# Three fp32r passes for the nearest Toeplitz tiles of a convolution, and where on the engines their operands are split

## The chip, the cores and the metric

The kernel runs on one core of a Trainium2 chip, in one launch. The metric is the time of the whole execution on the device, in microseconds (us). Five engines work side by side, each through its own instructions in order: TensorE (PE) multiplies matrices into PSUM, VectorE (DVE), ScalarE (ACT) and GpSimd (POOL) compute element by element, and SyncE (SP) issues DMA transfers.

## The reference, cut to what matters

```python
def reference(x, lengths, cond, ...):        # x: 32 batches, 64 channels, 1024 positions
    # 1. a long convolution per channel, by FFT, with a mask of lengths
    u_m = x * mask[:, None, :]
    K[h, l] = 2 * Re(sum_n Cs[h, n] * exp(dtA[h, n] * l))      # 64 modes, l = 0..1023
    y = irfft(rfft(u_m, n=2 * L) * rfft(K, n=2 * L), n=2 * L)[..., :L]
    y = (y + u_m * D[:, None]) * mask[:, None, :]
    # 2. grouped attention with rope on y: q, k, v products, softmax, output product
    x = x + attention(y, Wq, Wk, Wv, Wo)
    # 3. a product per batch with a chosen 64x64 matrix, then a feed-forward of experts
    return x + moe_lora(einsum("bct,bcd->bdt", x, W[cond]), W_base, gate_W, A, B)
```

Everything is float32. The change concerns part 1 alone.

## The kernel before

The convolution of a channel is a product with a Toeplitz matrix: y[t] is a sum of K[t - s] x[s]. Positions are cut into 8 blocks of 128; the tile of distance d (0 to 7) joins each block of x with the block d further on, and serves all (8 - d) x 32 columns (block and batch) at once. Each tile is cut into two halves c of 64 input positions. That makes 16 tiles (d, c), the list TILES; the nearer the distance, the more columns: 256, 256, 224, 224, 192, 192, and so on down to 32, 32.

**Steps.** The stage has 32 steps n of two channels each (S // 2). Channel r = 0 takes partitions 0 to 63 of the array's input, r = 1 takes 64 to 127, so that two matmuls run side by side. The first nine tiles are WIDE: 64 inputs x 128 outputs, two matmuls each (`wide`, L644). The other seven are NARROW: two halves of 64 outputs as well, four matmuls each (`narrow`, L654). All are fp32, which the trace shows as two records for each matmul. Even steps run WIDE and then NARROW, odd steps NARROW (and tile (0, 0) in narrow form) and then the rest of WIDE (`convolve`, L668). Four steps are a group (GP); kernels of the convolution are computed by groups.

**Rings.** Toeplitz rows of a step (`toep`, 544 columns) lie in a ring of three: SyncE may load those of step n when step n - 3 has ended (`load_toeplitz`, L615, four transfers; the rows come from `kpad` in DRAM, where ScalarE has stored the kernels). x of two steps (`xc`) lies in a ring of two, loaded ahead of the rows of an even step (`load_x_conv`, L587). PSUM has three slots. SyncE also loads a piece of the weights for the products that follow, in steps 5 to 16.

**Behind the matmuls of step n.** VectorE multiplies by the mask of lengths into `ym` (L740). ScalarE rounds it to fp32r into `y_hi` (L771, L772). GpSimd subtracts to get `y_lo` (L783, L784). Products later in the kernel run as three fp32r passes, high x high, high x low and low x high (PASSES), on such pairs.

**Kernels of the convolution**, two groups ahead, for the first six groups: GpSimd makes exponents (L392), VectorE phases after the mask of the group's first step (L463, L467, L474), ScalarE exponentials and sines in the second step, with a table load before each kind (L357, L373), VectorE tables in the third, TensorE the kernel product after the fourth (L543, in the first group within step 1 too), VectorE takes it out (`kernels_out`), and ScalarE stores it at the head of the group that follows (`store_kernels`, four DMA issues, L573).

The order on each engine is that in which the code is written: `conv_loads`, `conv_matmuls`, `conv_masks`, `conv_hi` and `conv_lo` each run their engine's loop over n. An engine that waits at one instruction runs none behind it.

## Time and profile before

| | |
|---|---|
| median of three runs | 877.52 us (876.6 to 879.48) |
| the profiled execution | 876.56 us, span 874.7 us |
| TensorE busy | 854.1 us (98%) |
| VectorE, ScalarE, GpSimd busy | 467.1, 221.4, 450.0 us |
| granted TensorE clock | 1.00 |
| convolution | up to 164.4 us of the span |

The profile is one execution. Busy time of TensorE counts overlapping records once, and says little of how near it is to its peak; the beat of a stage is read from when its pieces start, in the timeline. The chain of waits follows the work that ended last backward. A wait in it counts only if nothing else would have ended as late.

### The profile page before, as it was taken

The numbers are of one execution on the slowest core, as the hardware profiler recorded it, in microseconds if no ns is written. First come the engines' busy times: TensorE is split into PE (matmuls) and PEld (weight loads), VectorE is DVE, ScalarE is ACT, GpSimd is POOL, SyncE is SP. The second block draws the span as 40 slices with busy tenths as digits, with TensorE's granted clock in tenths as the row PEclk, the third lists the DMA queues.
The fourth block names the chain that finished last, engine by engine and source line by source line (L and its number), as shares of the span: only waits on it lengthen the run. The fifth ranks groups of instructions, "written<-read, shape, count | busy, mean of one in ns | idle before, by whom it ended". The sixth has DMA issues, their size and how long they took to land.

```text
span 874.7 us, 24616 instructions
## 1 busy us (share of the span) xinstructions
PE 854.1 (98%) x10866; PEld 741.9 (85%) x10866; DVE 467.1 (53%) x898; ACT 221.4 (25%) x377; POOL 450.0 (51%) x346
## 2 busy tenths in 40 slices
PE   3999999999999999999999999999999999999998
PEld 2899999988888888887777777777779999999998
DVE  7555651122522222238887777888854755545444
ACT  4445552100000000013132333333334322211220
POOL 3344555302367555649978888877746422102220
PEclk9999999999999999999999999999999999999999
DMA  3788877413354322255534454545437211222211
GB/s 95 177 207 220 208 186 196 162 60 127 109 183 129 82 74 73 50 166 154 142 129 149 135 176 165 173 163 173 151 123 234 96 59 57 83 97 97 98 49 49
DMA packets 97339, 114.90 MB, mean 131 GB/s; under 512 B 44112, under 2 KB 66896, under 8 KB 97232
## 3 DMA queue, kind: packets, MB, share of 16 engines
q1 hardware_dynamic: 94240, 112.29, 43.1%
q8 instruction: 86, 1.41, 0.7%
q10 hardware_dynamic: 2480, 0.51, 0.3%
q0 software_dynamic: 512, 0.53, 0.2%
q14 instruction: 21, 0.17, 0.1%
HBM read 80.16 MB, written 33.13 MB: 130 GB/s over the span
## 4 chain that ended last, share of the span: by engine, by line
PE 93%; SPq 3%; DMA 2%; DVE 1%; issue 0%; ACT 0%
PE ps L988 25%; PE ps L1275 21%; PE ps L1597 15%; PE ps L649 8%; PE ps L1625 5%; PE ps L952 5%; PE ps L660 4%; PE ps L1231 3%; PE ps L1211 3%; PE ps L1507 2%; SPq L606 2%; DMA toep<-kpad 2%; PE ps L1642 1%; PE ps L1641 1%; DMA kpad<-ksb 1%
## 5 line engine op out<-in xcount | busy, mean ns | idle before, releaser
L1597 PE MATMUL ps<-wb_hi,xf 128*128 128x424 f32 x440 | 127.0, 356 | 0.0
L988 PE MATMUL ps<-y_hi,w_hi 128*128 128x512 f32 x320 | 125.1, 391 | 0.0
L988 PE MATMUL ps<-y_hi,w_lo 128*128 128x512 f32 x320 | 124.5, 389 | 0.0
L988 PE MATMUL ps<-y_lo,w_hi 128*128 128x512 f32 x320 | 124.5, 389 | 0.0
L1573 POOL TENSOR_TENSOR xf<-xs,xf 128x512 fp32r<-128x512 f32 x32 | 42.1, 1347 | 124.8 <-DVE xs L1561 124.8
L1275 PE MATMUL ps<-y_hi 128*128 128x512 f32 x256 | 102.9, 402 | 0.0
L1275 PE MATMUL ps<-y_hi,y_lo 128*128 128x512 f32 x256 | 100.2, 391 | 0.0
L1275 PE MATMUL ps<-y_lo,y_hi 128*128 128x512 f32 x256 | 100.1, 391 | 0.0
L649 PE MATMUL ps<-xc,toep 64*128 64x192 f32 (+4 forms) x1088 | 97.1, 330 | 2.5 <-DMA toep<-kpad 2.4
L649 PEld LDWEIGHTS ps<-xc,toep 64*128 64x128 f32 x1088 | 91.2, 187 | 6.0 <-issue 3.8
L1597 PEld LDWEIGHTS ps<-wb_hi,xf 128*128 128x128 f32 x440 | 82.7, 188 | 2.3
L1100 POOL TENSOR_TENSOR rot<-rot,cst 128x512 f32<-128x512 f32 x40 | 52.8, 1319 | 58.7 <-DVE rot L1070 58.7
L1303 POOL TENSOR_TENSOR sc<-sc,stat 128x1024 f32<-128x1024 f32 x32 | 62.0, 1937 | 38.8 <-DVE stat L1299 38.8
L1597 PE MATMUL ps<-wb_lo,xf 128*128 128x424 f32 x220 | 77.6, 353 | 0.0
L1070 DVE LOAD_MASK_SELECT rot<-ps x40 | 0.6, 14 | 134.1 <-PE ps L988 119.1
L988 PEld LDWEIGHTS ps<-y_hi,w_hi 128*128 128x128 f32 x320 | 60.1, 188 | 12.8
L988 PEld LDWEIGHTS ps<-y_hi,w_lo 128*128 128x128 f32 x320 | 60.1, 188 | 12.5
L988 PEld LDWEIGHTS ps<-y_lo,w_hi 128*128 128x128 f32 x320 | 60.1, 188 | 12.3
L1317 POOL TENSOR_TENSOR sc<-sc,stat 128x1024 f32<-128x1024 f32 x32 | 66.8, 2086 | 2.2 <-DVE stat L1313 2.2
L783 POOL TENSOR_TENSOR y_lo<-ym,y_hi 128x256 fp32r<-128x256 f32 x32 | 30.3, 946 | 70.0 <-ACT y_hi L772 69.8
L1104 POOL TENSOR_TENSOR rf<-rot,rc 128x512 f32<-128x512 f32 x40 | 52.7, 1317 | 17.2 <-DMA k_rows<-rf 14.1
L820 ACT ACTIVATE w_hi<-wraw 128x1024 fp32r<-128x1024 f32 (+1 forms) x11 | 12.4, 1137 | 186.6 <-PE ps L988 108.8
(190 smaller groups left out, 1624.3 us busy)
## 6 DMA issues: line engine op xcount, KB each, us to landing
toep<-kpad SPq DMA_DIRECT2D x124, 136.0 KB
xc<-in_dram SPq DMA_DIRECT2D x32, 256.0 KB, 4.4
q_rows<-rf SPq DMA_DIRECT2D x32, 256.0 KB, 2.8
q<-q_rows SPq DMA_DIRECT2D x16, 512.0 KB, 3.9
xr<-in_dram SPq DMA_DIRECT2D x16, 512.0 KB, 4.4
x_scratch<-xr SPq DMA_DIRECT2D x16, 512.0 KB, 3.0
x<-x_scratch SPq DMA_DIRECT2D x16, 512.0 KB, 4.3
out_dram<-x SPq DMA_DIRECT2D x15, 512.0 KB, 2.9
```

Source lines behind the costliest of these rows:

```text
L649: mm = pe.matmul(ps[:, 2 * (n % 3) + r, d * NB:NJ * NB], toep[rows, n % TR, at:at + P], xc[rows, n // XH % XR, 1 - c, n % XH, 0:(NJ - d) * ...
L660: mm = pe.matmul(ps[half * HALF:(half + 1) * HALF, 2 * (n % 3) + r, d * NB:NJ * NB], toep[rows, n % TR, at:at + HALF], xc[rows, n // XH % ...
L952: mm = pe.matmul(out, wv[a][:, j, h * P:(h + 1) * P], y[b][:, j, b0:b1, s0:s1], start=(j == 0 and a + b == 0), stop=(j == NJ - 1 and a == 1))
L988: mm = pe.matmul(kq_bank(n), w[a][:, j, :], yt[b][:, j, g * 512:(g + 1) * 512], start=(j == 0 and a + b == 0), stop=(j == NJ - 1 and a == 1))
L1100: gp.tensor_tensor(r, r, across(C("sin"), 8), ALU.mult).then_inc(g_rsin, 1)
L1104: gp.tensor_tensor(rf[:, (NVB + n) % SR, :], rot[:, n % RR, :], rc[:, n % RR, :], ALU.add).then_inc(g_rsum, 1)
L1275: mm = pe.matmul(ps[:, 6 + n, :], heads, wo(c, t)[:, n, :], start=(at == 0), stop=(at == 3 * NQT - 1))
L1303: gp.tensor_tensor(sc_groups(u), sc_groups(u), along(stat[:, u % CR, 0, :], S), ALU.subtract).then_inc(g_sub, 1)
L1317: gp.tensor_tensor(sc_groups(u), sc_groups(u), along(stat[:, u % CR, 2, :], S), ALU.mult).then_inc(g_prob, 1)
L1573: gp.tensor_tensor(xf(i, op, 1)[:], xs(i, op), xf(i, op, 0)[:].bitcast(F32), ALU.subtract).then_inc(g_xflo, 1)
L1597: mm = pe.matmul(dst[:, PLAIN:], xf(i, idx, a)[:, t, :], wb(c, idx, t), start=(start and t == 0 and a + c == 0), stop=(t == 3 and a == 1), ...
L1625: mm = pe.matmul(plain_bank[:, k, :], xf(i, op, a)[:, t, :], w[c][:, first + t, :], start=(op in (A11, S1) and t + a + c == 0), stop=(op i ...
```

## The change

The four tiles of the two nearest distances (NEAR = 4: (0,0), (0,1), (1,0), (1,1)) run from step 2 on as three fp32r passes (`near_tiles`). For this, x and the first 320 columns of the Toeplitz rows of a step are split in two parts each. `near_hi` on ScalarE copies x (once `xc` has landed) and the rows (once `toep` has landed) to fp32r; `near_lo_x` on VectorE and `near_lo_rows` on GpSimd subtract. `near` holds two steps of rows, `xs_pair` two steps of x; the latter lies in the third slot of the split weights, and so the first key weights are loaded after the convolution. The scratch of the start shares memory with `near`.

The parts for step n + 2 are made in step n. For an odd n (and n = 0) they stand behind y_hi and y_lo of step n. For an even n from 2 on they stand ahead of mask, y_hi and y_lo of step n, and ScalarE waits there for `pe_near`, which TensorE raises after the near passes of step n. On TensorE the near passes stand between WIDE and NARROW in an even step, and at the end of an odd step.

Pieces of value weights are now loaded in steps 15 to 22 (W_FIRST = 16) and rounded in step 25; VectorE subtracts their low part, in steps 27 and 29, in place of GpSimd.

```diff
-        W_FIRST = 6
+        W_FIRST = 16
...
+        NEAR_COLS = 2 * P + HALF
+        near = [sb(f"near_{n}", [P, 2, NEAR_COLS], F32R, s1) for n in ("hi", "lo")]
...
+        xs_pair = [w[:, WR - 1, :].rearrange("p (r c n) -> p r c n", r=2, c=2) for w in wsp]
...
+        def near_tiles(pe, n):
+
+            pe.wait_ge(a_near, 2 * (n - FIRST_NEAR + 1))
+            pe.wait_ge(g_near, n - FIRST_NEAR + 1)
+            pe.wait_ge(v_near, n - FIRST_NEAR + 1)
+            for d, c in TILES[:NEAR]:
+                at = d * P + (1 - c) * HALF
+                for a, b in PASSES:
+                    for r in range(2):
+                        rows = slice(r * HALF, (r + 1) * HALF)
+                        mm = pe.matmul(ps[:, 2 * (n % 3) + r, d * NB:NJ * NB], near[a][rows, n % 2, at:at + P],
+                                       xs_pair[b][rows, n % 2, 1 - c, 0:(NJ - d) * NB],
+                                       start=False, stop=True, skip_group_check=True)
+            return mm
...
-            if n % 2 == 0:
+            if n >= FIRST_NEAR and n % 2 == 0:
+                for d, c in WIDE[NEAR:]:
+                    wide(pe, n, c, d, start=((d, c) == WIDE[NEAR]), stop=True)
+                near_tiles(pe, n).then_inc(pe_near, 1)
+                for d, c in NARROW:
+                    mm = narrow(pe, n, c, d, start=False, stop=True)
+            elif n >= FIRST_NEAR:
+                for d, c in NARROW:
+                    narrow(pe, n, c, d, start=((d, c) == NARROW[0]), stop=True)
+                for d, c in WIDE[NEAR:]:
+                    wide(pe, n, c, d, start=False, stop=True)
+                mm = near_tiles(pe, n)
+            elif n % 2 == 0:
...
+                if n + 1 == FIRST_NEAR or n % 2 == 0 and n >= FIRST_NEAR:
+                    near_lo_x(v, n + 1)
+                if near_early(n):
+                    near_lo_x(v, n + AHEAD)
+                if n in (W_FIRST + 11, W_FIRST + 13):
+                    value_weight_lo(v, (n - W_FIRST - 11) // 2)
                 v.wait_ge(pe_conv, n + 1)
...
+        def near_made(n):
+
+            return FIRST_NEAR <= n + AHEAD < S // 2
+
+        def near_early(n):
+
+            return near_made(n) and n % 2 == 0 and n >= FIRST_NEAR
+
+        def near_hi(act, n):
+            if near_early(n - AHEAD):
+                act.wait_ge(pe_near, (n - AHEAD - FIRST_NEAR) // 2 + 1)
+            act.wait_ge(ld_xc[n // XH % XR], 16 * 2 * (n // XH // XR + 1))
+            act.activation(xs_pair[0][:, n % 2, :, :], xc[:, n // XH % XR, :, n % XH, :], ACT.Copy).then_inc(a_near, 1)
+            act.wait_ge(ld_toep[n % TR], rows_landed(n))
+            act.activation(near[0][:, n % 2, :], toep[:, n % TR, 0:NEAR_COLS], ACT.Copy).then_inc(a_near, 1)
...
-                if n == W_FIRST + 13:
-                    weight_hi(act, 0)
+                if near_early(n):
+                    near_hi(act, n + AHEAD)
                 act.wait_ge(v_mask, n + 1)
                 act.activation(y_pair(0, n, 0), ym_pair(n, 0), ACT.Copy)
                 act.activation(y_pair(0, n, 1), ym_pair(n, 1), ACT.Copy).then_inc(a_yhi, 1)
+                if near_made(n) and not near_early(n):
+                    near_hi(act, n + AHEAD)
                 if n == 0:
                     store_kernels(act, 1)
...
+                if near_early(n):
+                    near_lo_rows(gp, n + AHEAD)
                 gp.wait_ge(a_yhi, n + 1)
                 gp.tensor_tensor(y_pair(1, n, 0), ym_pair(n, 0), y_pair(0, n, 0).bitcast(F32), ALU.subtract)
                 gp.tensor_tensor(y_pair(1, n, 1), ym_pair(n, 1), y_pair(0, n, 1).bitcast(F32), ALU.subtract).then_inc(g_ylo, 1)
...
+                if near_made(n) and not near_early(n):
+                    near_lo_rows(gp, n + AHEAD)
```

What stands in a row on ScalarE from the head of a group (step 8) to its second step. Before (L573 stores kernel rows, L771 and L772 are y_hi, L357 exponentials, L373 sines):

```order
L573 DMA kpad<-ksb 32x2x32 [waits v_k]
L573 DMA kpad<-ksb 32x2x32 x3
L771 ACTIVATE y_hi<-ym 128x256 [waits v_mask]
L772 ACTIVATE y_hi<-ym 128x256
L357 ACT_TABLE_LOAD
L357 ACTIVATE mg<-mg 128x256 [waits g_mag] x2
L373 ACT_TABLE_LOAD
L373 ACTIVATE rn<-rn,cst 128x256 [waits v_round]
L373 ACTIVATE rn<-rn,cst 128x256 x2
L771 ACTIVATE y_hi<-ym 128x256 [waits v_mask]
L772 ACTIVATE y_hi<-ym 128x256
```

And now, where L582 is the store, L843 and L844 are y_hi, L366 and L382 exponentials and sines, and L812 and L814 are the two copies of `near_hi`:

```order
L582 DMA kpad<-ksb 32x2x32 x3
L812 ACTIVATE w12_hi<-xc 128x512 [waits ld_xc1,pe_near]
L814 ACTIVATE near_hi<-toep 128x320 [waits ld_toep1]
L843 ACTIVATE y_hi<-ym 128x256 [waits v_mask]
L844 ACTIVATE y_hi<-ym 128x256
L366 ACT_TABLE_LOAD
L366 ACTIVATE mg<-mg 128x256 [waits g_mag] x2
L382 ACT_TABLE_LOAD
L382 ACTIVATE rn<-rn,cst 128x256 [waits v_round]
L382 ACTIVATE rn<-rn,cst 128x256 x2
L843 ACTIVATE y_hi<-ym 128x256 [waits v_mask]
L844 ACTIVATE y_hi<-ym 128x256
```

The copies for step 10 have come ahead of y_hi of step 8, with waits for two loads; those for step 11 stand behind y_hi of step 9. On GpSimd the same stretch, from the exponents (L401) on, where L823 is `near_lo_rows` and L859 and L860 are y_lo:

```order
L401 TENSOR_TENSOR mg<-t64,cst 128x256 [waits g_rtab,v_tab]
L401 TENSOR_TENSOR mg<-t64,cst 128x256
L823 TENSOR_TENSOR near_lo<-toep,near_hi 128x320 [waits a_near]
L859 TENSOR_TENSOR y_lo<-ym,y_hi 128x256 [waits a_yhi]
L860 TENSOR_TENSOR y_lo<-ym,y_hi 128x256
L859 TENSOR_TENSOR y_lo<-ym,y_hi 128x256 [waits a_yhi]
L860 TENSOR_TENSOR y_lo<-ym,y_hi 128x256
L823 TENSOR_TENSOR near_lo<-toep,near_hi 128x320 [waits a_near] x2
```

Before, the exponents and the y_lo pairs stood there alone; now the low rows of the odd step stand behind y_lo of the second step of the group.

## Rows read from the trace of the kernel before

**Rows 1.** The page, the chain that ended last: share of the span by engine
```profile
PE 93%; SPq 3%; DMA 2%; DVE 1%; issue 0%; ACT 0%
```

**Rows 2.** Timeline of PE: start us, length us, engine, line, operation, shapes, count
```profile
40.42 0.61 PE L543 MATMUL ps<-ph 64*128 64x128 f32 x8
...
68.09 3.31 PE L649 MATMUL ps<-xc,toep 64*128 64x256 f32 x36 [0.93 <-DMA toep<-kpad]
...
83.07 5.96 PE L649 MATMUL ps<-xc,toep 64*128 64x256 f32 x68
...
112.48 3.20 PE L649 MATMUL ps<-xc,toep 64*128 64x256 f32 x36
...
126.64 2.87 PE L649 MATMUL ps<-xc,toep 64*128 64x256 f32 x32
129.35 0.61 PE L543 MATMUL ps<-ph 64*128 64x128 f32 x8
129.80 3.20 PE L649 MATMUL ps<-xc,toep 64*128 64x256 f32 x36
...
161.53 2.87 PE L649 MATMUL ps<-xc,toep 64*128 64x256 f32 x32
```

**Rows 3.** Waits of PE from 28 to 170 us: sum, times, longest
```profile
PE ps L649 <- DMA toep<-kpad: 2.2, 3, 1.1
```

**Rows 4.** The chain in order of time: start us, length us, what
```profile
27.92 3.83 DMA toep<-kpad
...
138.44 0.63 SPq L593
...
141.71 5.21 DMA toep<-kpad
...
147.05 3.31 PE ps L649 x36
```

**Rows 5.** Timeline of ACT, steps 11 to 14, columns as in rows 2
```profile
77.56 0.65 ACT L771 ACTIVATE y_hi<-ym 128x256 fp32r<-128x256 f32 x1 [3.14 <-DVE ym L740]
78.02 0.64 ACT L772 ACTIVATE y_hi<-ym 128x256 fp32r<-128x256 f32 x1
78.56 2.91 ACTq L573 DMA_DIRECT2D kpad<-ksb  x4
...
83.62 1.28 ACT L357 ACT_TABLE_LOAD   x1
...
88.60 0.67 ACT L772 ACTIVATE y_hi<-ym 128x256 fp32r<-128x256 f32 x1
...
91.87 1.92 ACT L820 ACTIVATE w_hi<-wraw 128x2048 fp32r<-128x2048 f32 x1
```

**Rows 6.** Timelines of DVE (first line) and of POOL, same stretch
```profile
81.76 0.69 DVE L740 TENSOR_TENSOR ym<-ps,valid 128x512 f32<-128x512 f32 x1 [3.24 <-PE ps L660]
...
89.34 1.08 POOL L783 TENSOR_TENSOR y_lo<-ym,y_hi 128x256 fp32r<-128x256 f32 x1 [3.84 <-ACT y_hi L772]
90.36 0.95 POOL L784 TENSOR_TENSOR y_lo<-ym,y_hi 128x256 fp32r<-128x256 f32 x1
...
98.11 2.36 POOL L824 TENSOR_TENSOR w_lo<-wraw,w_hi 128x1024 fp32r<-128x1024 f32 x1
```

**Rows 7.** Timeline of PE, value products: the first and the last of 58
```profile
165.04 0.28 PE L952 MATMUL ps<-y_hi,w_lo 128*128 128x256 f32 x1
...
171.89 0.28 PE L952 MATMUL ps<-y_hi,w_lo 128*128 128x256 f32 x1
```

**Rows 8.** Timeline of ACT, steps 0 and 1
```profile
29.39 2.17 ACTq L573 DMA_DIRECT2D kpad<-ksb  x4
31.59 1.28 ACT L357 ACT_TABLE_LOAD   x1 [4.61 <-issue]
...
36.57 0.68 ACT L772 ACTIVATE y_hi<-ym 128x256 fp32r<-128x256 f32 x1
```

More of the change, by code:

```diff
@@ L155, in build @@
         ksb = sb("ksb", [P, 2, 2, GP * HB], F32, s1)
+        first = ExitStack()
+        prm = sb("prm", [P, 5, S], F32, first)
+        t64_first = sb("t64_first", [P, 18, S], F32, first)
+        first.close()
+        NEAR_COLS = 2 * P + HALF
+        near = [sb(f"near_{n}", [P, 2, NEAR_COLS], F32R, s1) for n in ("hi", "lo")]
         s1.close()
+        xs_pair = [w[:, WR - 1, :].rearrange("p (r c n) -> p r c n", r=2, c=2) for w in wsp]
         s2 = ExitStack()
@@ L288, in build @@
             "a_set", "v_set", "v_rho", "v_ang", "v_cs")]
-        g_zero, v_cidx, v_len, v_valid = [signal(n) for n in (
-            "g_zero", "v_cidx", "v_len", "v_valid")]
-        g_set, g_den, g_fac, g_rtab = [signal(n) for n in ("g_set", "g_den", "g_fac", "g_rtab")]
+        g_zero, v_cidx, v_valid = [signal(n) for n in (
+            "g_zero", "v_cidx", "v_valid")]
+        g_set, g_fac, g_rtab = [signal(n) for n in ("g_set", "g_fac", "g_rtab")]
         g_mag, a_mag, v_ph, v_round, a_sin, v_tab = [signal(n) for n in (
@@ L297, in build @@
             "pe_conv", "v_mask", "a_yhi", "g_ylo")]
-        a_whi, g_wlo, pe_unit = [signal(n) for n in (
-            "a_whi", "g_wlo", "pe_unit")]
+        pe_near, a_near, v_near, g_near = [signal(n) for n in (
+            "pe_near", "a_near", "v_near", "g_near")]
+        a_whi, g_wlo, v_wlo, pe_unit = [signal(n) for n in (
+            "a_whi", "g_wlo", "v_wlo", "pe_unit")]
         pe_v, v_v = signal("pe_v"), signal("v_v")
@@ L638, in conv_loads @@
                 part, piece = divmod(n - W_FIRST + 1, W_PIECES)
-                if 0 <= part < 3:
+                if 0 <= part < 2:
                     cols = slice(piece * W_COLS, (piece + 1) * W_COLS)
-                    source = w_v[:, part * NJ * P:(part + 1) * NJ * P] if part < 2 else w_qk[0]
-                    sp.dma_start(wraw[:, part, cols], source[:, cols]).then_inc(ld_w[part // 2 * 2], 16)
+                    source = w_v[:, part * NJ * P:(part + 1) * NJ * P]
+                    sp.dma_start(wraw[:, part, cols], source[:, cols]).then_inc(ld_w[0], 16)
         def wide(pe, n, c, d, start, stop=False):
@@ L650, in wide @@
                                xc[rows, n // XH % XR, 1 - c, n % XH, 0:(NJ - d) * NB],
-                               start=start, stop=stop)
+                               start=start, stop=stop, skip_group_check=(n >= FIRST_NEAR and not start))
             return mm
@@ L661, in narrow @@
                                    xc[rows, n // XH % XR, 1 - c, n % XH, 0:(NJ - d) * NB],
-                                   start=start, stop=stop)
+                                   start=start, stop=stop, skip_group_check=(n >= FIRST_NEAR and not start))
             return mm
@@ L666, in build @@
         WIDE, NARROW = TILES[:NJ + 1], TILES[NJ + 1:]
+        FIRST_NEAR = 2
+        AHEAD = 2
+        NEAR = 4
+        def near_tiles(pe, n):
[11 more added lines that the diff above has]
+            return mm
         def convolve(pe, n):
@@ L752, in ym_pair, with near_lo_x, near_lo_rows @@
             return ym[:, n % 2, i, :].rearrange("p (j b) -> p j b", b=NB)
+        def near_made(n):
[9 more added lines that the diff above has]
+            act.activation(near[0][:, n % 2, :], toep[:, n % TR, 0:NEAR_COLS], ACT.Copy).then_inc(a_near, 1)
+        def near_lo_x(v, n):
+            v.wait_ge(a_near, 2 * (n - FIRST_NEAR) + 1)
+            v.tensor_tensor(xs_pair[1][:, n % 2, :, :], xc[:, n // XH % XR, :, n % XH, :],
+                            xs_pair[0][:, n % 2, :, :].bitcast(F32), ALU.subtract).then_inc(v_near, 1)
+        def near_lo_rows(gp, n):
+            gp.wait_ge(a_near, 2 * (n - FIRST_NEAR) + 2)
+            gp.tensor_tensor(near[1][:, n % 2, :], toep[:, n % TR, 0:NEAR_COLS],
+                             near[0][:, n % 2, :].bitcast(F32), ALU.subtract).then_inc(g_near, 1)
         def conv_hi(act):
@@ L799, in w_loaded @@
             s = w_slot(m).start
-            pieces = (2 * W_PIECES, 0, W_PIECES)[s]
-            whole = 0 if m <= 0 else (m - 1) // WR + 1 if s == 0 else m // WR + (s == 1)
+            pieces = (2 * W_PIECES, 0, 0)[s]
+            whole = 0 if m < 0 else (m - 1) // WR + 1 if s == 0 else m // WR + 1
             eng.wait_ge(ld_w[s], 16 * (pieces + whole))
@@ L811, in load_weights @@
             if w_users(m) > 0:
-                sp.wait_ge(g_wlo, w_users(m))
+                sp.wait_ge(v_wlo, 2)
+            if w_users(m) > 1:
+                sp.wait_ge(g_wlo, w_users(m) - 1)
             s = w_slot(m).start
@@ L820, in weight_hi, with value_weight_lo @@
             act.activation(wsp[0][:, w_slot(m), :], wraw[:, w_slot(m), :], ACT.Copy).then_inc(a_whi, 1)
-        def value_weight_lo(gp, part):
-            gp.wait_ge(a_whi, 1)
-            return gp.tensor_tensor(wsp[1][:, part, :], wraw[:, part, :], wsp[0][:, part, :].bitcast(F32), ALU.subtract)
+        def value_weight_lo(v, part):
+            v.wait_ge(a_whi, 1)
+            v.tensor_tensor(wsp[1][:, part, :], wraw[:, part, :], wsp[0][:, part, :].bitcast(F32), ALU.subtract).then_inc(v_wlo, 1)
         def weight_lo(gp, m):
@@ L884, in qkv_transfers @@
         def qkv_transfers(sp):
+            load_weights(sp, 0)
             load_weights(sp, 1)
```

33 lines of the change are left out of this document (14 added, 19 removed).

## The prediction

> **What bounds the kernel now.** I read first the chain of work that ended last: TensorE holds nearly all of it [rows 1], and the convolution is its stretch up to 164.4 us. The timeline of TensorE gives that stretch its beat [rows 2]. One group of four steps is the time from one kernel-row product (L543, which follows the last step of a group) to the next: 40.42 to 129.35 holds five groups, (129.35 - 40.42) / 5 = 17.8 us each, and a pair of steps takes some 8.65 us. TensorE is almost never idle there: its waits in the whole stage sum to 2.2 us, none over 1.1 [rows 3]. So the stage looks bound by matmuls. But two things stand close behind. The rows of a Toeplitz tile for step n+2 are asked for when step n-1 ends and land 8.5 us later (138.44 to 141.71 + 5.21 = 146.92, step 28 starts at 147.05) [rows 4]: a pair of steps shorter than that waits for its load. And ScalarE does, in the second step of each group of the first six, the tables, exponentials and sines of the kernels two groups on: from 83.62 to 88.60 + 0.67 = 89.27 it holds y_hi of step 13 back, 5.65 us in all; the subtractions of GpSimd for that step follow until 91.31 [rows 5, 6]. In the kernel before nobody waits for that: y_lo is needed only two steps later.
>
> **What TensorE gains.** Per step from 2 on, four wide fp32 tiles (256, 256, 224, 224 columns, 960 in sum, two row halves side by side) go, and 24 fp32r matmuls come: 12 pairs. Old price: 68 records over 3328 columns take 5.96 us [rows 2], so 960 columns take 1.72 at most; four cycles a column at 2.4 GHz are 1.60. I take 1.64. New price: no fp32r matmul on half rows stands in the trace. The nearest row is the one on full rows, 256 columns: from 165.04 to 171.89 lie 57 of them, 0.120 us apart, that is 106.7 ns of columns and 13 ns more [rows 7]. If the two halves overlap as the fp32 ones do, the pass costs 3 x (2 x 0.120 + 2 x 0.107) = 1.36; without the 13 ns 1.20. If they don't overlap, 2.72. I take 1.36, since the fp32 tiles of this very shape do run as pairs. The gain is 0.28 a step, 1.1 us a group, 8.4 us over 30 steps if nothing else spoke.
>
> **What the split costs on the other engines.** Each step adds on ScalarE a copy of 512 columns and one of 320 (from 1.92 us for 2048 columns and 0.65 for 256 strided ones [rows 5]: about 0.6 and 0.45), on VectorE one subtraction of 512 columns (as the mask, 0.69 [rows 6]), on GpSimd one of 320 (2.36 us for 1024 [rows 6], so 0.74). Their busy time fits. Their place doesn't. On ScalarE the copies for an even step n+2 stand ahead of y_hi of step n, and the second waits for the Toeplitz rows of n+2. Those land 7.1 to 8.5 us after step n-1 ended (3.27 of issuing, then the 3.83 to 5.21 us of landing shown [rows 4]), about when step n+2 starts. ScalarE stands still until then; in the kernel before y_hi of step n ran just as step n ended. Behind it are queued, in the same order: y_hi of n, the tables, exponentials and sines, y_hi of n+1, and only then the copies for the odd step n+3; on GpSimd y_lo of n+1 stands ahead of the low part of those rows. TensorE needs that low part in the fourth step of the group.
>
> I follow this ring for a group, from the end e of the step before it (4g-1):
> - The mask and y_hi of 4g-1 (0.7 + 1.1), copies for 4g+1 (1.0), four stores of kernel rows (2.9 [rows 5]) fill ScalarE until e + 5.8; then the copy of x for 4g+2, VectorE's subtraction and the mask of step 4g end at e + 7.9. The rows land at e + 7.1 to 8.5 and are copied 0.5 later. So y_hi of 4g starts between e + 7.9 and e + 9.0. I take 8.3, below the middle: while step 4g-1 waits, its loads and those before it have landed, and the transfers have less to share with.
> - y_hi of 4g: 1.10 (77.56 to 78.66). Tables to y_hi of 4g+1: 5.65. [rows 5]
> - y_lo of 4g+1: 1.97 (89.34 to 91.31) [rows 6], and 0.07 of signal.
> - Low part of the rows of 4g+3: 0.74 + 0.05. Near passes of 4g+3, which end the step: 1.36 + 0.05.
>
> Sum: 8.3 + 1.10 + 5.65 + 2.04 + 0.79 + 1.41 = **19.3 us a group** (18.8 to 20.2), against 17.8 before. TensorE's own work would be 17.3 less 1.1 (the group 112.48 to 129.80 is one without a wait), 16.2 to 16.6; it waits about 3 us in the fourth step, ahead of its near passes. Since the ring is longer than the matmuls, their gain doesn't count in it but for the pass at its end.
>
> **The start.** The copies for step 2 stand ahead of the store of the second group of kernel rows, and their rows land at 27.92 + 3.83 = 31.75 [rows 4]. ScalarE then goes on at 32.25; the stores (2.17, begun at 29.39 before) end at 34.45, tables to y_hi of step 1 take 31.59 to 36.57 + 0.68 = 5.66, to 40.1 [rows 8]; y_lo of step 1 as above 2.04, to 42.1; low rows of step 3 to 42.9, near passes to 44.35. Step 3 ended at some 40.6 before (the kernel product behind it stands at 40.42 [rows 2]): +3.8 us. The kernel rows of group 1 are stored 2.9 us later, and so the rows of step 4 land 2.9 later; that hides in it.
>
> **The rest of the stage.** After step 23 there are no exponentials and sines left. Eight steps took 161.53 + 2.87 = 164.4 less 126.64 + 2.87 = 129.5, that is 34.9 [rows 2]; less 8 x 0.28 is 32.6, but a pair of 8.08 us stands against a load of up to 8.5, and a load that is asked for a pair ahead holds two pairs to their mean, (8.08 + 8.5) / 2 = 8.3: 33.2. The rounding of the value weights (1.92) falls in step 25; the ring of that group, 8.3 + 1.1 + 1.9 + 1.1 + 2.0 + 0.8 + 1.4 = 16.6, just ties with matmuls. Gain -1.6. Weight pieces of other steps, and the first key weights, now loaded after the convolution, lie under the 44 us of value products; the change leaves y of step 31 as far ahead of its reader as it was.
>
> **Sum.** End of step 3 +3.8; five groups 5 x (19.3 - 17.8) = +7.6; the last eight steps -1.6: **+9.8 us**. The profiled execution took 876.56 (span 874.7 and 1.9 around it), the median of the runs shown is 877.52, 1 us over it. The span comes to 884.5, the median to 877.5 + 9.8 = **887.3 us**.
>
> **Rivals.**
> 1. *The beat is TensorE's after all* (faster). If the rows landed some 3 us earlier than here, or if ScalarE had 3 us less, the ring would be below 16.4 and each pair bound by matmuls or loads: 15 pairs, 8.65 down to 8.3, and the first group 1 to 2 us late: 877.5 - 5.3 + 1 = 873 us. For it: TensorE's own work does shrink. Against: it takes 3 us out of a ring of which each term but the first has a row. It decides at a ring of 17.8. Chance 0.11. Between, with a ring of about 17.6 to 18.4 (copies and landings all at their short end): 876 to 881, chance 0.09.
> 2. *The halves don't overlap.* Near pass 2.72: a step takes 4.33 - 1.64 + 2.72 = 5.4, a group 21.7 with its kernel product, which beats the ring (20.7). Step 3 ends 1.4 later, five groups 5 x 3.9 = 19.5, the last eight 8 x 1.08 = 8.7: 877.5 + 5.2 + 19.5 + 8.7 = 911. Against: the fp32 pairs of this shape. Chance 0.06. The Trainium skill ("TensorE: Matmul & The Clock Gate", LDWEIGHTS and "The mechanism") gives a load of 128 columns 107 ns and lets it overlap a running matmul where the row group differs; by that each half would alternate load and matmul, some 0.2 us a pair, and the time would be near this rival's. The rows on full rows speak against it: 0.120 us from one fp32r matmul to the next, each with a weight load of its own [rows 7].
> 3. *The clock.* TensorE now stands idle 3 to 4.5 us once a group; the longest wait of the stage before was 1.1 us [rows 3], at clock 1.00. If the clock falls from 2.4 to 1.2 GHz, the near pass behind the gap doubles, +1.4 us on the ring, while the slower steps after it fit in the slack; at most six times 1.4, 896 us. Chance 0.10. The same page of the skill says that idle TensorE is throttled to half rate; no row of this trace shows it either way.
> 4. *Same*, by cases that cancel: within rival 1's middle.
>
> **Chances.** Forecast (ring 18.4 to 20.2, 882 to 893) 0.64, rival 1 0.11, its middle 0.09, rival 2 0.06, rival 3 0.10. What a measurement tells from no change is 0.3%, 2.6 us. Faster 0.11, same 0.07, slower 0.82. The range of 8 in 10 takes the forecast, the clock up to 896 and the middle down to 879: 879 to 896.
>
> **What would show it.** In the changed profile: TensorE's wait in the fourth step of groups 0 to 5, ahead of the near passes, on GpSimd's low rows, some 3 us, and 4 in step 3; none later. ScalarE's copy of near rows for even steps waiting for the load for 1 to 3 us. L552 to L552 19.3 us instead of 17.8. Near passes of 24 matmuls in 1.36 us. Wrong if the gaps are missing (then rival 1), if the passes take 2.7 us, or if a clock under 1.00 stands in the slices.

## The result, and the profile after

The changed kernel took 899.57 us (median of 4 runs, 898.39 to 904.24), beside 877.62 us for the kernel before (median of 4): the ratio is 1.025, with an interval of 1.021 to 1.029. That is 22 us slower, and 3.6 us above the upper end of the range. The execution that was profiled took 904.24 us, the longest of the four, with a span of 901.9. The kernel was run and profiled once more later on (`again` below: 897.88 us, its profiled span 895.1), and where the two profiles differ both are given.

The waits of TensorE from 20 to 200 us (sum, times, longest), to be held against [rows 3]:

```profile
PE ps L691 <- POOL near_lo L823: 16.3, 5, 4.5
PE ps L669 <- issue: 3.8, 2, 2.8
PE ps L658 <- DMA toep<-kpad: 1.6, 2, 1.3
PE ps L691 <- issue: 1.4, 1, 1.4
```

Before, no wait of the stage was longer than 1.1 us, and all were for a load. Now TensorE waits five times, 16.3 us in sum, for the low part of the Toeplitz rows that GpSimd makes (L823), and each of these waits stands ahead of the near passes (L691) in the fourth step of a group. This is the gap that the prediction places there. The waits named "issue", for which the profile finds no releaser, are new, and they are of two kinds. The one at L691 (1.4 us) is the sixth wait for low rows: TensorE goes on at 64.61, 0.07 us after GpSimd's low rows end, as it does behind the other five. Those at L669 stand inside runs of narrow matmuls, where no semaphore is waited for; the part on `inter` below takes them up.

The chain of one group in order of time (start, length, what), to be held against [rows 4] and [rows 5]. The group starts at e = 108.75, where the kernel product ahead of it begins:

```profile
109.03 0.63 SPq L602
...
112.29 4.55 DMA toep<-kpad
...
116.86 0.47 ACT near_hi L814
117.33 0.58 ACT y_hi L843
...
118.39 1.28 ACT L366
...
119.68 0.73 ACT mg L366 x2
...
120.43 1.28 ACT L382
...
121.72 1.31 ACT rn L382 x3
...
124.09 1.09 POOL y_lo L859
125.19 1.30 POOL y_lo L860
126.49 1.27 POOL near_lo L823
...
127.85 2.91 PE ps L691 x24
```

The order is that of the ring, link by link: the loads are issued when the fourth step ends, the last rows land at e + 8.1, near_hi (the copy of the rows) is followed by y_hi, the table loads, exponentials and sines, y_hi of the next step, y_lo and low rows on GpSimd, and then the 24 near matmuls. These took 2.91 us here; where TensorE ran at full clock they took 1.45 to 1.55 (from their first start to the start of what follows).

The page's row of the granted clock (tenths of full speed in 40 slices of 22.5 us) shows two slices below the others in the convolution; before, all forty were alike:

```profile
PEclk9999998989999999999999999999999999999999
```

At the finer grain of the trace the clock goes down to 1.2 GHz six times between 42 and 193 us, for 3.4 or 6.8 us each, 30.7 us in sum: once at the end of each of the five waits of the first row or just behind it, and once behind this wait in the midst of the narrow matmuls of the last steps (start, length, line; the idle time ahead in brackets):

```profile
181.78 2.02 PE L669 MATMUL ps<-xc,toep 64*64 64x128 f32 x94
186.57 0.74 PE L669 MATMUL ps<-xc,toep 64*64 64x64 f32 x18 [2.77 <-issue]
```

In `again` the same kernel spent 17.1 us at 1.2 GHz in four places, behind gaps of 4.5, 2.6, 4.2 and 2.5 us but not behind those of 1.4 and 1.8, and had no such stall in its last steps. The starts of the kernel products (L552) there give the length of the groups, as in [rows 2]:

```profile
46.14 1.11 PE L552 MATMUL ps<-ph 64*128 64x128 f32 x8
...
66.05 0.65 PE L552 MATMUL ps<-ph 64*128 64x128 f32 x8
...
87.57 1.15 PE L552 MATMUL ps<-ph 64*128 64x128 f32 x8
...
107.41 0.65 PE L552 MATMUL ps<-ph 64*128 64x128 f32 x8
...
128.50 1.15 PE L552 MATMUL ps<-ph 64*128 64x128 f32 x8
...
149.51 1.15 PE L552 MATMUL ps<-ph 64*128 64x128 f32 x8
```

| us | before | forecast | after | again |
|---|---|---|---|---|
| end of step 3 (start of L552) | 40.4 | 44.35 | 46.4 | 46.1 |
| a group, mean of five | 17.8 | 19.3 | 21.1 | 20.7 |
| last eight steps | 34.8 | 33.2 | 40.6 | 34.5 |
| span | 874.7 | 884.5 | 901.9 | 895.1 |

For `again`: 5.7 + 5 x 2.9 - 0.3 = 19.9 us of the 20.4 us between the spans. So all but 0.5 us is found inside the convolution.

### The profile page after: what moved, and what is told of

Its sections match the earlier page's. It is cut to its first block, busy times and chain, and to the rows that moved or that the text cites. A ratio compares the mean times of both kernels' runs of the same rounds, so it can differ in the third digit from the quotient of the medians.

```text
span 901.9 us, 25138 instructions
## 1 busy us (share of the span) xinstructions
PE 860.9 (95%) x11046; PEld 751.4 (83%) x11046; DVE 502.3 (56%) x930; ACT 249.5 (28%) x437; POOL 483.1 (54%) x374
## 4 chain that ended last, share of the span: by engine, by line
PE 85%; DMA 4%; ACT 4%; SPq 3%; POOL 2%; DVE 1%; issue 1%; ACTq 0%
PE ps L1063 24%; PE ps L1352 20%; PE ps L1674 14%; PE ps L1702 5%; PE ps L1027 5%; PE ps L691 3%; PE ps L1308 3%; PE ps L1288 3%; DMA toep<-kpad 3%; PE ps L658 2%; PE ps L1584 2%; SPq L615 2%; PE ps L669 1%; PE ps L1719 1%; PE ps L1718 1%
## 5 line engine op out<-in xcount | busy, mean ns | idle before, releaser
L658 PE MATMUL ps<-xc,toep 64*128 64x192 f32 (+4 forms) x668 | 61.2, 330 | 1.6 <-DMA toep<-kpad 1.6
L658 PEld LDWEIGHTS ps<-xc,toep 64*128 64x128 f32 x668 | 56.7, 204 | 3.3 <-issue 2.6
L1845 DVE TENSOR_TENSOR x<-ps,x 128x424 f32<-128x424 f32 (+1 forms) x64 | 40.3, 642 | 33.9 <-PE ps L1674 31.8
```

Source lines behind the costliest of these rows:

```text
L658: mm = pe.matmul(ps[:, 2 * (n % 3) + r, d * NB:NJ * NB], toep[rows, n % TR, at:at + P], xc[rows, n // XH % XR, 1 - c, n % XH, 0:(NJ - d) * ...
L1845: v.tensor_tensor(x, src[:, first:], x, ALU.add).then_inc(v_sum_out, 1)
```

## The experiments

Each kernel ran beside the kernel before on its chip. "Over before" is the ratio less one, times 877.5 us, so that rows of different chips can be compared. The last three columns are read from the profiled execution as in the table above; that of `nosplit_spread` was the longest of its six, 885.4 us beside a median of 880.0.

| kernel | us | ratio [interval] | over before | end of step 3 | group | last eight |
|---|---|---|---|---|---|---|
| changed kernel | 899.6 | 1.025 [1.021, 1.029] | +21.9 | 46.4 | 21.1 | 40.6 |
| again | 897.9 | 1.0247 [1.0221, 1.0274] | +21.7 | 46.1 | 20.7 | 34.5 |
| late | 895.0 | 1.0214 [1.0166, 1.0261] | +18.8 | 45.1 | 20.0 | 36.8 |
| copy | 892.6 | 1.014 [1.0088, 1.0191] | +12.3 | 42.9 | 19.5 | 40.7 |
| nolowx | 897.3 | 1.0229 [1.0205, 1.0253] | +20.1 | 45.4 | 20.1 | 38.8 |
| fill | 901.0 | 1.0284 [1.023, 1.0338] | +24.9 | 45.7 | 21.7 | 34.2 |
| fill4 | 899.1 | 1.0264 [1.0243, 1.0286] | +23.2 | 45.0 | 21.4 | 34.1 |
| fill3 | 900.1 | 1.0256 [1.0236, 1.0276] | +22.5 | 44.9 | 20.7 | 34.7 |
| nosplit | 882.9 | 1.0077 [1.0053, 1.01] | +6.8 | 45.6 | 17.4 | 35.4 |
| nosplit_spread | 880.0 | 1.0041 [1.0021, 1.0062] | +3.6 | 45.9 | 17.8 | 37.3 |
| inter | 886.1 | 1.0097 [1.0061, 1.0133] | +8.5 | 40.5 | 19.5 | 35.7 |
| spread | 882.9 | 1.008 [1.006, 1.01] | +7.0 | 41.8 | 18.8 | 33.5 |
| spread2 | 886.3 | 1.0082 [1.0053, 1.011] | +7.2 | 40.5 | 19.4 | 35.2 |
| cut | 907.6 | 1.0357 [1.0339, 1.0374] | +31.3 | 44.2 | 21.7 | 43.1 |

### Is the splitting the cause: nosplit

```diff
+            made = min(n - FIRST_NEAR + 1, 2)
...
+            pe.wait_ge(g_near, made)
...
         def near_made(n):
...
-            return FIRST_NEAR <= n + AHEAD < S // 2
+            return FIRST_NEAR <= n + AHEAD < FIRST_NEAR + 2
...
         def near_early(n):
...
-            return near_made(n) and n % 2 == 0 and n >= FIRST_NEAR
+            return False
```

> The changed kernel with the fp32r operands made for steps 2 and 3 alone and used again in all later steps, so the products of the near distances are those of other data: ScalarE, VectorE and GpSimd do no splitting from step 4 on, TensorE's work is the same. Ring theory: without the copies the ring is shorter than TensorE's work; no wait for low rows, the clock stays at 1.00, 15 pairs at 8.3 us, 873 us (871 to 877). Rival (TensorE's own new work, its instruction supply or the loads set the beat): waits named issue stay and it is near 895 to 899.

It took 882.9 us, 6.8 over before, where the ring theory said 873 (871 to 877) and its rival 895 or more: neither number. The waits of TensorE:

```profile
PE ps L692 <- POOL near_lo L822: 4.0, 1, 4.0
PE ps L658 <- DMA toep<-kpad: 3.3, 5, 1.0
PE ps L669 <- issue: 2.0, 3, 1.3
```

TensorE does all its new work here, and 15 of the 22 us are gone: the splitting on the other engines costs them. The wait for low rows is left in step 3 alone, whose operands are still made (end of step 3 at 45.6, +5.2). From there on a group takes 17.4 us. The matmuls of a pair of steps run in 7.94 us (wide 1.34 and 1.44, near 1.55 and 1.45, narrow 2.16 together, taken from the trace) against 8.43 before, so four steps and the kernel product could be done in 16.4. The loads and the waits named issue keep the rest: what TensorE saves turns mostly into waits. So even without any splitting the change would be worth 2 us over the five groups, where rival 1, with 0.35 us a pair, has 3.5.

### Which link of the ring: late, copy, nolowx

`late` puts the splits of even steps behind y_hi and y_lo as well, the half of the change that its title names second undone (the low part of x moves with them):

```diff
-                if n + 1 == FIRST_NEAR or n % 2 == 0 and n >= FIRST_NEAR:
+                if near_made(n - 1):
                     near_lo_x(v, n + 1)
-                if near_early(n):
-                    near_lo_x(v, n + AHEAD)
...
         def near_early(n):
-            return near_made(n) and n % 2 == 0 and n >= FIRST_NEAR
+            return False
```

> The changed kernel, but the splits for every step, even or odd, stand behind the high and low part of y (the other half of the change's title undone; the wait on the near passes goes with it). Ring theory: ScalarE makes y_hi of step 4g before it waits for the rows of step 4g+2, so the ring is shorter by one y_hi, 1.1 us: about 20.0 us a group instead of 21.1, 893 us (888 to 896). The wait for GpSimd's low rows in the fourth step stays, some 2 us. Rival (the beat is TensorE's or the loads'): no change, 899.

895.0 us. By time alone it is not told apart from the changed kernel (the intervals of the ratios overlap); by the trace it is. y_hi of step 4g starts at e + 5.4 (e + 6.8 in the first of the five groups) instead of 8.4, the low rows are ready at e + 17.9 on the mean, against 18.97 in `again`, and the group is 0.7 us shorter (20.0, as forecast). TensorE's waits are divided among several causes, none over 1.9 us but the one in step 3:

```profile
PE ps L691 <- DVE w_lo L816: 5.6, 5, 1.5
PE ps L669 <- issue: 5.2, 3, 1.9
PE ps L691 <- POOL near_lo L821: 3.9, 1, 3.9
PE ps L691 <- issue: 2.8, 4, 1.0
```

`copy` makes plain copies of the exponentials and sines of groups 2 to 7, which leaves the table loads out:

```diff
-                act.activation(mg[:, i, :], mg[:, i, :], ACT.Exp).then_inc(a_mag, 1)
+                act.activation(mg[:, i, :], mg[:, i, :], ACT.Copy if g >= 2 else ACT.Exp).then_inc(a_mag, 1)
...
+                if step > 2:
+                    act.activation(rn[:, i, part], rn[:, i, part], ACT.Copy).then_inc(a_sin, 1)
```

> The changed kernel with the exponentials and sines of groups 2 to 7 replaced by plain copies on ScalarE, so no function tables are loaded there (two loads of 1.28 us a group) and the later kernel rows are wrong numbers. Ring theory: 2.6 us less between y_hi of 4g and y_hi of 4g+1, the low rows of 4g+3 ready at e + 16.3 instead of 18.9, the pass behind them at 2.4 GHz 1.55 us: 18.0 us a group instead of 21.1, and 2.6 less before step 3: 884 us (880 to 889). Rival (the ring isn't ScalarE's; loads or instruction supply set 20 us a group): 893 or more.

892.6 us, 9.6 us less than the changed kernel by the ratios where 15.6 were forecast: above the theory's range, which ended at 889, and close to the 893 of its rival. The start gained 3.2 us. In a group the low rows were ready at e + 17.6, not 16.3, because ScalarE now waits for VectorE (its timeline, with the idle time in brackets):

```profile
90.73 0.72 ACT L366 ACTIVATE mg<-mg 128x256 f32<-128x256 f32 x2
93.51 1.03 ACT L383 ACTIVATE rn<-rn 128x256 f32<-128x256 f32 x3 [2.05 <-DVE rn L486]
```

The sines need the phases that VectorE makes behind the mask of 4g, and the mask stands behind the low part of x for 4g+2, which waits for a load. In the changed kernel these phases end at 121.04, 0.7 us before ScalarE has its second table loaded (120.43 + 1.28, in the chain above). Take the loads away, and VectorE is the link in their place. So ScalarE's tables are one link of the ring, and not the only one that sets its length.

`nolowx` takes VectorE's added subtractions away from step 4 on, and TensorE's wait for them:

```diff
-            pe.wait_ge(v_near, n - FIRST_NEAR + 1)
+            pe.wait_ge(v_near, min(n - FIRST_NEAR + 1, 2))
...
-                if n + 1 == FIRST_NEAR or n % 2 == 0 and n >= FIRST_NEAR:
+                if n + 1 == FIRST_NEAR or n == 2:
                     near_lo_x(v, n + 1)
-                if near_early(n):
-                    near_lo_x(v, n + AHEAD)
```

> The changed kernel without VectorE's low part of x from step 4 on (that of steps 2 and 3 is used again, so the third product of the near passes is of other data). In the changed kernel VectorE makes the low parts of x for 4g+3 and 4g+4 while GpSimd makes y_lo of 4g+1 and the low rows, and these take 2.42 and 1.31 us where the forecast had 2.04 and 0.79. Contention theory: 1.97 and 0.87 again, the low rows ready at e + 18.1 instead of 18.95, 19.9 us a group, 895 us (893 to 897). If GpSimd's operations take that long by themselves: 899.

The timelines of GpSimd and, last row, of VectorE in `again`, where y_lo of 4g+1 (L859, L860) and two low rows (L823) run beside two low parts of x:

```profile
123.12 1.08 POOL L859 TENSOR_TENSOR y_lo<-ym,y_hi 128x256 fp32r<-128x256 f32 x1 [3.95 <-ACT y_hi L844]
124.15 1.35 POOL L860 TENSOR_TENSOR y_lo<-ym,y_hi 128x256 fp32r<-128x256 f32 x1
125.46 2.14 POOL L823 TENSOR_TENSOR near_lo<-toep,near_hi 128x320 fp32r<-128x320 f32 x2
...
123.51 2.55 DVE L818 TENSOR_TENSOR w_lo<-xc,w_hi 128x512 fp32r<-128x512 f32 x2
```

And GpSimd in `nolowx` (y_lo L857 and L858, low rows L821):

```profile
119.92 1.07 POOL L857 TENSOR_TENSOR y_lo<-ym,y_hi 128x256 fp32r<-128x256 f32 x1 [3.83 <-ACT y_hi L842]
120.94 0.90 POOL L858 TENSOR_TENSOR y_lo<-ym,y_hi 128x256 fp32r<-128x256 f32 x1
121.79 0.87 POOL L821 TENSOR_TENSOR near_lo<-toep,near_hi 128x320 fp32r<-128x320 f32 x1
```

y_lo takes 1.94 us instead of 2.4, the low rows 0.87 instead of 1.3 (means of five groups), and these are ready at e + 18.1, as forecast. The contention is shown: the same instruction on GpSimd takes up to 1.5 times as long while VectorE subtracts. A group takes 20.1 us: the low rows come 0.9 us earlier than in `again`, but the near passes behind them took 1.9 us instead of 1.6 (two of five ran at 1.2 GHz), so that 0.5 us a group is left. By the ratios the time fell by 1.6 us (their intervals overlap) against the forecast's 4, and 897.3 lies just outside the forecast 893 to 897: in its profiled execution 2.8 us were lost to a stall in the last steps like that at 186.57 above.

### The clock: fill, fill4, fill3

Dummy matmuls ahead of the wait keep TensorE at work in the gap (3, 4 or 6 of them, more in step 3):

```diff
         def near_tiles(pe, n):
+            if n % GP == 3 and n // GP + 2 < NHG:
+                for _ in range(5 if n == 3 else 3):
+                    pe.matmul(ps[:, 7, 2 * P:4 * P], C("ident"), cst[:, 0:2 * P], start=True, stop=True)
             pe.wait_ge(a_near, 2 * (n - FIRST_NEAR + 1))
```

> The changed kernel with 6 dummy fp32 matmuls of 256 columns (9 in step 3), some 0.43 us each, ahead of the wait for the near operands in steps 3, 7, ..., 23; they fill the gap and write to unused columns of a bank. Clock theory: the gap itself stays (TensorE is late by as much), but the near pass behind it and the wide matmuls of the next step run at 2.4 GHz: near pass 1.4 us instead of 2.4 to 2.9, a group about 19.7 instead of 21.1, 891 us (888 to 894). If the clock costs nothing that the slack doesn't take, 899; if the dummies are longer than the gap, more.

> As fill, with 4 dummy matmuls (8 in step 3) instead of 6 (9). In fill the low rows were ready 0.1 to 2.8 us before the dummies ended (mean 0.9 us), so that it paid for the clock with dummies. Clock theory: the ring with TensorE at 2.4 GHz is 20.1 us a group (fill: 18.5 to 19.5 from the kernel product to the low rows, and 1.55), 1.0 less than the changed kernel's 21.1: 894 us (891 to 897). If the low clock costs nothing by itself: 899.

> As fill4, with 3 dummy matmuls (5 in step 3), 1.3 us, so that they end before the low rows are ready and a gap of 1.5 us or so is left (the order late had gaps of that size with the clock at 2.4 GHz). Dummies cost nothing then. Clock theory: near pass behind the gap 1.55 us instead of 2.4 to 2.9, a group 20.3 instead of 21.1, 895 us, 4 to 6 below the changed kernel run beside it. Rival (the clock's cost lies in the slack, or is given back by the loads): within 1.5 us of the changed kernel beside it.

> The changed kernel once more, beside fill3. Both theories: 899 to 900 us, low rows of 4g+3 ready at e + 18.9, six gaps of 3 us or more, the clock at half speed behind each of them.

`fill3` took 900.1 us and the changed kernel beside it 897.9 (0.8 us apart by the ratios, 2.2 by the medians, where the rival had said 1.5 at most); `fill4` and `fill` gave 899.1 and 901.0. The clock theory's 891 to 895 is out: no time came back. `again` itself met its forecast in the low rows (e + 18.97) and came 1 us below it in time; its gaps were not six of 3 us or more, but 4.5, 1.4, 2.6, 1.8, 4.2 and 2.5. The waits of `fill3`:

```profile
PE ps L694 <- POOL near_lo L826: 4.3, 2, 2.3
PE ps L669 <- issue: 3.4, 3, 1.3
PE ps L694 <- issue: 3.0, 4, 1.3
```

The dummies fill what was a wait of 15.8 us in `again`. TensorE spends 6.8 us at 1.2 GHz in the stage here, 3.4 in `fill` and in `fill4`, 17.1 to 30.7 in the changed kernel. The gap in step 3 shows the price at full size, since its near passes take 2.68 us in `again` (43.46 to 46.14) and step 3 ends 1.2 us earlier in `fill3`. In the groups `fill3` is no shorter (20.7 and 20.7): in `again` the near passes behind the gap took 1.4 to 1.9 us, since the clock fell late in them or after them; in the profile of 904.24 us three of five took 2.1 to 2.7. And with dummies y_hi of 4g, which follows the copy of rows, started later, at e + 8.6 to 9.1 on the mean of each kernel, against 8.4; why is open. In `fill` the dummies also held the near passes back, by up to 2.7 us after the low rows were ready. So the lower clock is a consequence of the gap. By the near passes themselves it costs 1.2 us in step 3 and, over the five groups, 0.6 us in `again` and 3 us in the longer execution; what it costs in the steps behind them isn't separated here, since the dummies moved other things too. It isn't what made the kernel 22 us slower.

### A better order, and the waits named issue: inter, spread, spread2

`inter` orders the same work so that no link of the ring is late; VectorE and GpSimd are reordered to match. On ScalarE:

```diff
+                g, k = n // GP, n % GP
+                if k == 0 and n > 0:
+                    x_hi(act, n + 2)
+                if k == 1:
+                    if near_made(n):
+                        x_hi(act, n + 2)
+                    if g + 2 < NHG:
+                        sines(act, step_of(g + 2))
+                    if near_made(n):
+                        rows_hi(act, n + 2)
...
                 act.wait_ge(v_mask, n + 1)
                 act.activation(y_pair(0, n, 0), ym_pair(n, 0), ACT.Copy)
                 act.activation(y_pair(0, n, 1), ym_pair(n, 1), ACT.Copy).then_inc(a_yhi, 1)
...
+                if k == 0:
...
+                    rows_hi(act, n + 2)
+                    if g + 2 < NHG:
+                        magnitudes(act, g + 2)
...
+                if k == 3 and near_made(n):
+                    x_hi(act, n + 2)
+                    if g + 2 < NHG:
+                        store_kernels(act, g + 2)
+                    rows_hi(act, n + 2)
```

> Same work as the changed kernel in another order: ScalarE makes y_hi of step 4g ahead of the copy of the rows of 4g+2, the exponentials follow, the rows of 4g+3 are copied between the sines and y_hi of 4g+1, the kernel rows are stored after y_hi of 4g+3; GpSimd makes the low rows of 4g+3 ahead of y_lo of 4g+1. By the ring theory each near operand is then ready within 1 us of its use: a group 16.9 to 17.8 us, 875 us (872 to 880). If the copies cost what they cost wherever they stand (ScalarE's or VectorE's sum of work), 890 to 899.

886.1 us: 13 of the 22 us are back, which is what the place of the new work in the queues cost, but the time is 11 us above the forecast for this kernel. The longest waits are now these:

```profile
PE ps L669 <- issue: 6.0, 5, 2.1
PE ps L552 <- DVE ph L521: 3.2, 3, 1.8
```

The longest of them, on TensorE's timeline, stands in the middle of the narrow matmuls of one step, where no semaphore is waited for:

```profile
44.80 0.91 PE L669 MATMUL ps<-xc,toep 64*64 64x32 f32 x31
...
47.83 0.82 PE L669 MATMUL ps<-xc,toep 64*64 64x96 f32 x37 [2.12 <-issue]
```

TensorE's records (matmuls, weight loads, and its sequencer's waits for semaphores) counted from the start of the kernel tell where such stalls stand. In the ten profiles in which the narrow matmuls of an even and an odd step follow each other with fp32r near passes around them, 27 stalls of over 0.3 us lie inside a run of narrow matmuls, and all 27 begin at a record whose number is 193 above a multiple of 256: 1217, 2497, 4545 and 5313 in `inter`, 2497 and 6593 in the changed kernel, 2497 in `again`. The six other stalls of that length inside a run of wide or near matmuls stand at the same number. In each of these traces the instruction queue q8 moves one packet of 16,384 bytes for every 256 of these records. This is the window of the DMA from 44.9 to 46.4 us in `inter`, just ahead of the stall that ends at 47.83 (busy tenths in 40 slices, then the queue's packets, MB and share):

```profile
DMA  9959989899939919796676995949995997959919
...
q8 instruction: 1, 0.02, 5.5%
```

The packet began at 44.95, 4.5 us after TensorE had passed the spot one block earlier (record 961, at 40.49), ended at 46.28, and the next record started 1.5 us later. So it is in all 27 stalls: the last packet ahead of them began 1.7 to 6.1 us after the spot one block earlier was passed, and TensorE went on 1.1 to 1.6 us after that packet had ended, however long the stall. The DMA engines are at 90% or more in 24 of the 40 slices. In the kernel before, such packets began 0.7 to 3.1 us after the spot was passed, and no block stalled. `spread` tests this reading. It puts wide, narrow and near in this order in each step, so that a block of 256 records never holds two steps' narrow matmuls in a row:

```diff
             if n >= FIRST_NEAR:
                 for d, c in WIDE[NEAR:]:
                     wide(pe, n, c, d, start=((d, c) == WIDE[NEAR]), stop=True)
                 for d, c in NARROW:
                     narrow(pe, n, c, d, start=False, stop=True)
                 mm = near_tiles(pe, n)
```

> The order of inter, and on TensorE each step from 2 on in the order wide, narrow, near pass, so that the narrow matmuls of two steps no longer stand together. In inter 112 narrow matmuls with 112 weight loads run in 2.16 us, and its waits named issue (6.8 us in the stage) fall in or behind them, four of the five longest exactly where the count of TensorE's records from the start is 193 above a multiple of 256; a packet of the instruction queue of 16 KB (256 instructions of 64 bytes) begins up to 5.3 us after the spot one block before is passed. Supply theory: 256 records then never run in less than 4.4 us (3.3 in inter), the waits named issue fall from 6.8 to 0 to 3 us, near passes of even steps need their operands 1.1 us later, 879 us (875 to 883). Rival (the waits are a matter of the loads or of semaphores the profile doesn't name): as inter, 886.

```profile
PE ps L552 <- DVE ph L521: 4.7, 4, 1.7
PE ps L658 <- DMA toep<-kpad: 2.7, 3, 1.5
PE ps L669 <- DMA toep<-kpad: 1.5, 1, 1.5
PE ps L691 <- issue: 0.3, 1, 0.3
```

The stalls are gone: none at 193 of 256, and the waits named issue fall from 6.8 us to 0.3. The time is 882.9 us, 1.5 below `inter` by the ratios, whose intervals overlap, and 4 above the forecast of 879. The new order has its own price (a pair of steps takes 8.26 us of matmuls instead of 7.94), and VectorE's tables now hold up the kernel product. The last eight steps take 33.5 us, close to the 33.2 of the prediction. `nosplit_spread` does the same to `nosplit`:

> nosplit (fp32r operands made for steps 2 and 3 alone and used again, so the near products are those of other data) with the order wide, narrow, near pass in every step. Supply theory: no waits named issue, 880 us instead of 882.9 (878 to 883); what is left over 873 is the wait in step 3 (4.0 us) and the loads. If the loads alone hold the pairs at 8.7 us: 883.

880.0 us, as the supply theory said: no stall at 193 of 256, and 3.2 us faster than `nosplit` by the ratios, with intervals that overlap slightly. `spread2` moves VectorE's phases ahead of the low part of x, its tables a step forward, and ScalarE's y_hi of 4g ahead of its copy of x:

```diff
+                if k == 0 and g + 2 < NHG:
+                    phases(v, step_of(g + 2))
                 if k == 0 and near_made(n):
                     near_lo_x(v, n + 2)
-                if k == 0 and g + 2 < NHG:
-                    phases(v, step_of(g + 2))
```

> The order of spread, with VectorE's phases ahead of its low part of x for step 4g+2, its tables a step earlier, and ScalarE's y_hi of 4g ahead of its copy of x for 4g+2. In spread the kernel product waited four times for the tables (4.7 us), because the phases stood behind a low part of x that waited for a load. If that wait is what is left, groups go from 18.8 to 17.5 us, 877 us (874 to 881), which would be no better than before. If loads take its place, as spread, 883.

Neither theory's number: 886.3 us, the same as `spread` by the ratio. The kernel product waits no more, but the near passes of 4g+1 and 4g+2 each wait about 1 us: the first for its rows, whose copy stands behind the stores of kernel rows on ScalarE's queue, the second for the low part of x, now behind the phases on VectorE. The profile names 6.9 us of these waits issue, yet they are no stalls of supply: they stand ahead of near passes, 0.07 us behind the end of the low rows or 0.12 behind that of the low part of x, and none is at 193 of 256. No version here beats the kernel before.

### More records on the kernel before: cut

```diff
+                parts = (0, 3, 6, NJ - d) if n >= 2 and d < 2 else (0, NJ - d)
+                for lo, hi in zip(parts, parts[1:]):
+                    mm = pe.matmul(ps[:, 2 * (n % 3) + r, (d + lo) * NB:(d + hi) * NB], toep[rows, n % TR, at:at + P],
+                                   xc[rows, n // XH % XR, 1 - c, n % XH, lo * NB:hi * NB],
...
```

> The kernel before, its four near wide fp32 tiles of every step from 2 on cut into three column pieces each: same columns, same fp32, no splits on the other engines, but 244 records of TensorE a step instead of 190 (the changed kernel has 200 in a shorter step). Supply theory: waits named issue appear, of 1 to 3 us each at blocks of 256, 5 to 15 of them, 886 us (880 to 895). Rival (the number of instructions costs nothing): 877 to 879.

907.6 us, far above both, and without a single wait named issue. So it did not test the supply: TensorE itself became slower and left the fetches time. Its timeline for a pair of steps (124 wide records, then 120 narrow):

```profile
73.67 8.19 PE L651 MATMUL ps<-xc,toep 64*128 64x96 f32 x124
81.79 2.66 PE L662 MATMUL ps<-xc,toep 64*64 64x128 f32 x120
```

[rows 2] have 68 wide records over the same columns (83.07). From their start to that of the narrow ones the trace has 5.90 us there and 8.12 here, 2.22 us for 56 more records, 40 ns each. Cutting a fp32 matmul by columns isn't free at pieces of 96, 64 and 32 columns.

## Why the prediction was wrong in size

Sign, place and mechanism were right: TensorE waits in the fourth step of each group for GpSimd's low rows, behind a ring through ScalarE's queue, and its own gain doesn't count. By the prediction's own steps, with means of five groups of `again`:

| term of the ring | forecast | measured |
|---|---|---|
| e to y_hi of 4g | 8.3 | 8.4 |
| y_hi of 4g and to the end of y_hi of 4g+1 | 1.10 + 5.65 | 6.8 |
| y_lo of 4g+1 | 2.04 | 2.46 |
| low rows of 4g+3 | 0.79 | 1.26 |
| near passes, to the next kernel product | 1.41 | 1.7 |
| sum | 19.3 | 20.7 |

- **What failed is the two terms on GpSimd**, 0.9 of 1.4 us a group, 4.5 us in all. They were taken from [rows 6] of the kernel before, where no subtraction of VectorE runs beside them (its mask product does, 0.69 us from 90.25, and the y_lo beside it took 0.95), or by columns from one instruction. The change itself adds two subtractions on VectorE that run at that moment. Without them, in `nolowx`, y_lo took 1.94 us instead of 2.4 and the low rows 0.87 instead of 1.3. The prediction put the added subtractions under "their busy time fits" and did not ask what they do to a neighbour.
- **The near passes** were forecast at 1.36 us and took 1.45 to 1.55, 0.117 to 0.13 us a pair: the halves overlap, rival 2 is out. The Trainium skill ("TensorE: Matmul & The Clock Gate", "LDWEIGHTS") gives a weight load its columns divided by 1.2 in ns, 107 for 128 columns; an estimate from it, with load and matmul in turn on each half, is 0.2 us a pair. The trace disagrees.
- **The start** was short by 1.8 to 2.0 us: 0.9 on GpSimd, 1.3 for the near passes of step 3 at the lower clock (2.68 for 1.36), less 0.5 since y_hi of step 1 ended at 39.6 and not at 40.1. Rival 3 had this mechanism and gave it 0.10; the granted clock was below 1.00 (0.983 to 0.990) in every execution of the changed kernel on record. The clock falls about the end of the gap, as the forecast of that rival says. The Trainium skill ("TensorE: Matmul & The Clock Gate", "What's actually happening") has the same of an idle TensorE, and the trace agrees: in `again` TensorE waits from 38.9 to 43.5 and is at 1.2 GHz from 42.7 on. The price of the lower clock in the groups was put at 1.4 us each; the near passes behind the gap took 1.6 us on the mean in `again` and 2.1 in the longer execution, against 1.5 at full clock, and the time of `fill3` shows none of it back.
- **The last eight steps** were to gain 1.6 us. They gained 0.3 in `again` and lost 5.8 in the profile of after. Loads and the ring hold them, and TensorE's instruction fetch, which is no term of the prediction at all, took 2.8 to 3.3 us there in three of the profiles (after, `copy`, `nolowx`) and 1.0 to 2.0 at a time in five more (`late`, `nosplit`, `inter`, `fill3`, `fill4`).
- **Range.** The sum reached 896 by the clock alone. The cases were treated as exclusive, a longer ring or a lower clock; both came together, since the one causes the other.

What stays open: why the rows of 4g+2 are copied later when dummies fill the gap, and what sets the delay of an instruction fetch. That it has to do with loads ahead of it is argued from the busy DMA engines, not shown. What `spread`, `spread2` and `nosplit_spread` show is that the stalls go when the narrow matmuls are spread out.

## What to carry to other kernels

When an edit puts new operations beside old ones on VectorE and GpSimd, the old durations don't hold: price the pair as it will run together. An operation that waits for a load, put into an in-order queue ahead of work that others need, lengthens the ring for everyone behind it, and the engine that was to gain can pay once more in clock behind the gap. A faster TensorE also asks for its instructions faster: look for a dense run of short matmuls, and keep two such runs apart.

## What the runs showed of the hardware

- GpSimd's subtraction of 320 columns takes 0.87 us alone and 1.3 beside a VectorE subtraction; VectorE's of 512 columns takes 0.69 alone and up to 1.4 beside it (1.28 each in the rows of `again` above).
- TensorE's instructions come in packets of 16,384 bytes for 256 of its records; where the records ran out before the next packet was there, TensorE stood idle for up to 3.3 us and went on 1.1 to 1.6 us after the packet's end (27 stalls).
- fp32r matmuls of 256 columns on two row halves, each with a weight load, run as pairs, 0.12 us from pair to pair; at 1.2 GHz 0.21.
- Each of the 19 idle gaps of 2.5 to 4.6 us that TensorE has in the convolutions of these profiles came with 3.4 or 6.8 us at 1.2 GHz, which began between 1.4 us before its end and 1.4 us behind it. Of the shorter gaps some did (1.75 us up to 99.95 in `inter`) and some didn't (1.8 us up to 105.95 and 1.4 up to 64.6 in `again`).
- fp32 matmuls cut into pieces of 96, 64 and 32 columns on a row half cost 40 ns for each record that the cut adds.
